# Attention of a four-stage transformer block: one written order of steps, or three

## The reference

```python
q, k, v = x @ wq, x @ wk, x @ wv             # 32 query heads, 8 key and value heads, 32 wide
q, k = rope(q), rope(k)                      # two layouts of the rotation, one per layer
scores = einsum('bqhd,bkhd->bhqk', q, k) / sqrt(32) + causal_mask
attn = softmax(scores, axis=-1)
out = einsum('bhqk,bkhd->bqhd', attn, v).reshape(b, s, 1024) @ wo
```

## Time and profile before

| | us |
|---|---|
| three runs | 3035.17, 3039.46, 3039.74 |
| median | 3039.46 |
| the profiled execution | 3036.84 |
| its span, first to last instruction | 3035.1 |
| TensorE busy | 2620.5 (86%) |
| VectorE busy | 1819.1 (60%) |
| ScalarE, GpSimd busy | 1081.8, 1123.2 |
| mean granted TensorE clock | 0.935 |

### The profile page before, as it was taken

The page is one execution under the profiler, slowest core; times in us unless marked ns, Lnnn a source line. Parts: engine busy times, 40 slices in busy tenths (PEclk is TensorE's granted clock), DMA queues, the critical chain, the costliest instruction groups (busy, mean ns, idle before and its releaser), DMA issues. The chain is left out here.

```text
span 3035.1 us, 50649 instructions
## 1 busy us (share of the span) xinstructions
PE 2620.5 (86%) x15056; PEld 1810.9 (60%) x15056; DVE 1819.1 (60%) x4485; ACT 1081.8 (36%) x2317; POOL 1123.2 (37%) x801
## 2 busy tenths in 40 slices
PE   7799997889998799653768999988799996996999
PEld 6556653655654588542645555545556553885887
DVE  5577775547776433688764666764577774225453
ACT  2155454135555211352511445552155454002000
POOL 7265653445664100000043555636265552001111
PEclk9999998999999899766979999989899998998999
DMA  4223221323231421000233323222323223433111
GB/s 149 87 81 104 64 75 63 117 71 104 77 86 42 161 69 55 0 0 7 83 132 95 106 61 93 73 83 74 90 81 103 64 75 112 146 131 146 63 69 42
DMA packets 121079, 252.95 MB, mean 83 GB/s; under 512 B 12720, under 2 KB 39728, under 8 KB 120880
## 3 DMA queue, kind: packets, MB, share of 16 engines
q1 hardware_dynamic: 120912, 251.03, 25.9%
HBM read 166.57 MB, written 84.41 MB: 83 GB/s over the span
## 5 line engine op out<-in xcount | busy, mean ns | idle before, releaser
L605 ACT ACTIVATE a_prob<-a_pst 128x512 f32<-128x512 f32 (+3 forms) x1536 | 660.7, 493 | 581.8 <-PE a_pst L886 576.2
L698 DVE CUSTOM_DVE_ANT_0 a_psh<-a_psh,a_edge 128x128 f32<-128x128 f32 (+3 forms) x1024 | 479.5, 518 | 247.7 <-PE a_psh L839 218.8
L839 PE MATMUL a_psh<-a_kst,a_qst 127*128 127x512 f32 (+3 forms) x1536 | 494.6, 371 | 79.4 <-DMA a_qst<-q 52.7
L886 PE MATMUL a_pst<-a_qst,a_kst 128*128 128x512 f32 (+2 forms) x1536 | 490.1, 374 | 22.7 <-DMA a_qst<-rowmax 17.8
L509 POOL TENSOR_TENSOR a_prob<-a_prob 128x2048 f32<-128x2048 f32 (+1 forms) x96 | 405.6, 4226 | 241.6 <-PE a_ppv L902 241.6
L839 PEld LDWEIGHTS a_psh<-a_kst,a_qst 127*128 127x128 f32 x1536 | 272.1, 191 | 321.9 <-DVE a_mx L701 104.7
L701 DVE TENSOR_REDUCE a_mx<-a_psh 128x1 f32<-128x512 f32 x512 | 328.2, 685 | 117.3 <-PE a_psh L839 116.4
L886 PEld LDWEIGHTS a_pst<-a_qst,a_kst 128*128 128x128 f32 x1536 | 289.4, 195 | 164.2 <-ACT a_prob L605 105.0
L902 PE MATMUL a_ppv<-a_prob,a_vg 128*32 128x512 f32 (+3 forms) x3072 | 319.8, 503 | 0.0
L915 PE MATMUL a_pden<-a_prob,a_ones 128*32 128x512 f32 (+3 forms) x2304 | 220.4, 475 | 13.8 <-POOL a_prob L509 13.8
L494 POOL TENSOR_SCALAR_AFFINE_SELECT a_prob<-a_prob 128x512 f32<-128x512 f32 x256 | 162.4, 640 | 184.7 <-ACT a_prob L605 184.3
(11 more groups left out here) (228 smaller groups left out, 4222.5 us busy)
## 6 DMA issues: line engine op xcount, KB each, us to landing
a_qst<-q SPq DMA_DIRECT2D x192, 256.0 KB, 4.4
a_wraw<-in_wqkv SPq DMA_DIRECT2D x52, 512.0 KB, 4.3
q<-a_stg_hi SPq DMA_DIRECT2D x64, 256.0 KB, 2.1
q<-a_stg_lo SPq DMA_DIRECT2D x64, 256.0 KB, 2.4
a_kst<-kT SPq DMA_DIRECT2D x96, 128.0 KB, 2.6
oT<-a_oT SPq DMA_DIRECT2D x32, 256.0 KB, 2.4
oT<-a_vT SPq DMA_DIRECT2D x32, 256.0 KB, 2.9
h_oraw<-oT SPq DMA_DIRECT2D x16, 512.0 KB, 4.0
```

The lines of the kernel that those rows point to most:

```text
L605: act.activation(prob[k % len(prob)][:, h, off:], pst[:, (k * GH + h) % 3, off:], ACT.Exp, scale=scale).then_inc(s["exp_done"], 1)
L698: part = dve.tensor_tensor_reduce(scores, scores, edge[:, BANK - n:], 1.0, 2 * MASKED, ALU.add, ALU.max, mx_hq[kc][:, h, qt:qt + 1])
L839: mm = pe.matmul(psh[:, at, i * n:(i + 1) * n], qst[par][0:P - 1, h, qt * P:(qt + 1) * P], kst[par][0:P - 1, kc * BANK:kc * BANK + n], sta ...
L886: pe.matmul(pst[:, (k * GH + h) % 3, off:], kst[par][:, ki * P:(ki + 1) * P], qst[par][:, h, qc * BANK + off:(qc + 1) * BANK], start=True, ...
```

## The change

Three orders are written out in place of one: `ORDER` for the looped groups, `ORDER_6` for group 6 and `ORDER_7` for group 7. `body7` is now `ORDER_7` without its `X` and `P` steps. Each list holds the same steps as before, in other places; no instruction, tile or semaphore is added or removed. `iteration` goes, `iterations` returns the lists, `parsed` reads `n` as the next batch and lets a list have no `S`.

In `ORDER`, `NORM:0` moves from behind `P:1.3` at the group's end to behind `ST:6.3`, the seventh key tile; the `S` start behind `P:0.0`; `ST:11.3` stands ahead of `P:1.1`; `VG` and `NORM:1` come a few steps earlier. In `ORDER_6` four `S` stand ahead of `ST:0.0`, and `NORM:0` at the end of unit 7. In `ORDER_7` `XL:0` to `XL:3` spread over the first units, each of the x steps has a written place, `NORM:0` stands in unit 10, and all eight `P:n` come at the end, behind `D:11`.

```diff
--- before.py
+++ after.py
@@ -75,39 +75,72 @@
 
 
 ORDER = """
-    P:0.0 P:0.1
-    ST:0.0 WL ST:0.1 ST:0.2 S P:0.2 ST:0.3 P:0.3
-    ST:1.0 ST:1.1 P:0.4 ST:1.2 S HI:1 ST:1.3 P:0.5
-    ST:2.0 ST:2.1 P:0.6 LO:1 S P:0.7 ST:2.2 S ST:2.3
-    ST:3.0 V:0 D:0 S S ST:3.1 ST:3.2 S ST:3.3 V:1
-    ST:4.0 ST:4.1 RS:1 ST:4.2 HI:0 S S D:1 ST:4.3 LO:0
-    ST:5.0 S ST:5.1 S V:2 V:3 D:2 D:3 S ST:5.2 S ST:5.3 S V:4 S
-    ST:6.0 S S ST:6.1 ST:6.2 S ST:6.3 V:5
-    ST:7.0 S ST:7.1 SUM:4+5 S ST:7.2 S ST:7.3 S V:6 SUM:6+7 D:4+5 S
-    ST:8.0 S ST:8.1 S RS:0 ST:8.2 S ST:8.3 S
-    ST:9.0 V:7 S S ST:9.1 ST:9.2 ST:9.3 S D:6+7 S
-    ST:10.0 ST:10.1 S V:8 S SUM:8+9 ST:10.2 S ST:10.3 V:9 S
-    ST:11.0 S ST:11.1 ST:11.2 P:1.0 P:1.1 ST:11.3 S P:1.2 S D:8+9 WS V:10 V:11 RK D:10 D:11 MT P:1.3
-      NORM:0 P:1.4 P:1.5 P:1.6 P:1.7 NORM:1 VG
+    P:0.0 S P:0.1
+    ST:0.0 WL ST:0.1 ST:0.2 S P:0.2 S ST:0.3
+    ST:1.0 P:0.3 S ST:1.1 P:0.4 HI:1 S P:0.5 ST:1.2 LO:1 ST:1.3
+    ST:2.0 S P:0.6 S ST:2.1 P:0.7 S ST:2.2 ST:2.3
+    ST:3.0 V:0 D:0 V:1 RS:1 ST:3.1 ST:3.2 S ST:3.3 S S
+    ST:4.0 HI:0 ST:4.1 ST:4.2 D:1 V:2 ST:4.3 S S
+    ST:5.0 S ST:5.1 D:2 V:3 S S ST:5.2 ST:5.3 LO:0 S
+    ST:6.0 D:3 V:4 S ST:6.1 S ST:6.2 ST:6.3 NORM:0 V:5 SUM:4+5
+    ST:7.0 S S ST:7.1 S ST:7.2 ST:7.3 V:6 D:4+5
+    ST:8.0 SUM:6+7 S RS:0 ST:8.1 ST:8.2 S S ST:8.3 S
+    ST:9.0 V:7 S ST:9.1 ST:9.2 S S ST:9.3 D:6+7
+    ST:10.0 S S V:8 SUM:8+9 ST:10.1 S S ST:10.2 V:9 S ST:10.3
+    ST:11.0 S ST:11.1 P:1.0 ST:11.2 S ST:11.3 P:1.1 RK S WS P:1.2 S D:8+9 V:10 V:11 D:10 D:11 MT P:1.3 VG
+      P:1.4 P:1.5 NORM:1 P:1.6 P:1.7
 """
 
+ORDER_6 = """
+    S S S S
+    ST:0.0 ST:0.1 ST:0.2 ST:0.3 HI:1
+    ST:1.0 S ST:1.1 ST:1.2 S S LO:1 S V:0 ST:1.3 S
+    ST:2.0 ST:2.1 D:0 ST:2.2 ST:2.3
+    ST:3.0 V:1 ST:3.1 S ST:3.2 ST:3.3 D:1
+    ST:4.0 V:2 RS:1 ST:4.1 S ST:4.2 ST:4.3 D:2 V:3 S
+    ST:5.0 ST:5.1 S S ST:5.2 D:3 S ST:5.3 S
+    ST:6.0 ST:6.1 S S V:4 S ST:6.2 S ST:6.3 S
+    ST:7.0 S S ST:7.1 ST:7.2 SUM:4+5 ST:7.3 V:5 V:6 SUM:6+7 D:4+5 NORM:0
+    ST:8.0 S ST:8.1 S ST:8.2 S ST:8.3 S
+    ST:9.0 V:7 ST:9.1 S ST:9.2 S ST:9.3 S D:6+7 V:8 S S
+    ST:10.0 S ST:10.1 ST:10.2 SUM:8+9 V:9 S ST:10.3 S S S
+    ST:11.0 ST:11.1 ST:11.2 S ST:11.3 V:10 D:8+9 D:10 V:11 D:11 MT NORM:1
+"""
+
+ORDER_7 = """
+    ST:0.0 ST:0.1 ST:0.2 XL:0 ST:0.3 XL:1
+    ST:1.0 ST:1.1 ST:1.2 ST:1.3 V:0 XL:2
+    ST:2.0 ST:2.1 ST:2.2 XS:0 XS:1 XN:0 V:1 ST:2.3
+    ST:3.0 XS:2 ST:3.1 ST:3.2 ST:3.3 XT:0 XL:3 D:0 XN:1 XC:0 XN:2 V:2
+    ST:4.0 D:1 ST:4.1 ST:4.2 XS:3 XT:1 XC:1 D:2 XL:4 V:3 ST:4.3
+    ST:5.0 ST:5.1 XS:4 XL:5 D:3 XT:2 XN:3 XC:2 ST:5.2 V:4 XN:4 ST:5.3 SUM:4+5
+    ST:6.0 ST:6.1 ST:6.2 XS:5 XT:3 XL:6 XC:3 ST:6.3
+    ST:7.0 V:5 ST:7.1 XS:6 XL:7 XN:5 XT:4 XC:4 ST:7.2 ST:7.3 D:4+5 V:6 XN:6
+    ST:8.0 SUM:6+7 ST:8.1 XT:5 XS:7 XC:5 ST:8.2 V:7 XN:7 ST:8.3
+    ST:9.0 ST:9.1 ST:9.2 XT:6 XC:6 ST:9.3 D:6+7 V:8
+    ST:10.0 ST:10.1 NORM:0 ST:10.2 SUM:8+9 ST:10.3
+    ST:11.0 ST:11.1 XT:7 XC:7 ST:11.2 ST:11.3 V:9 D:8+9 V:10 D:10 V:11 D:11 P:n.0 NORM:1 P:n.1 P:n.2
+      P:n.3 P:n.4 P:n.5 P:n.6 P:n.7
+"""
+
 
 def parsed(text):
 
 
     steps, k = [], 0
+    number = lambda x: "next" if x == "n" else int(x)
     for word in text.split():
         what, _, rest = word.partition(":")
         if what == "S":
             steps.append(("S", k))
             k += 1
         elif what in ("ST", "P"):
-            steps.append((what, *(int(x) for x in rest.split("."))))
+            steps.append((what, *(number(x) for x in rest.split("."))))
         elif what in ("D", "SUM"):
             steps.append((what, tuple(int(x) for x in rest.split("+"))))
         else:
             steps.append((what, int(rest or 0)))
-    assert k == len(USES)
+    assert k in (0, len(USES))
     return steps
 
 
@@ -118,42 +151,17 @@
 SUMS = [step[1] for step in STEPS if step[0] == "SUM"]
 
 
-def iteration(full_s=True, proj=True, ahead=False):
-
-
-
-
-    left_out = set() if proj else {"P", "WL", "WS", "RK", "VG"}
-    if not full_s:
-        left_out |= {"S", "MT"}
-    order = []
-    for step in STEPS:
-        what, k = step[:2]
-        if what in ("HI", "LO", "RS") and not (proj if k == 0 else full_s):
-            continue
-        if what not in left_out:
-            order.append(step)
-    if ahead:
-
-
-        def put(step, *others):
-            order[order.index(step) + 1:order.index(step) + 1] = others
-
-        for i in range(PIECES):
-            put(("ST", 11, 1) if i < 3 else ("ST", 11, 3) if i < 6 else ("V", 10), ("P", "next", i))
-        for i in range(ST_):
-            put(max([("ST", i + 1, 0)] + [("XN", i - 2)] * (i > 1) + [("XC", i - 4)] * (i > 3), key=order.index), ("XS", i))
-            put(max(("V", i), ("XS", i), key=order.index), ("XN", i))
-            put(max([("ST", i + 3, 1), ("XN", i)] + [("XC", i - 1)] * (i > 0), key=order.index), ("XT", i))
-            late = max(("V", i + 2), ("XT", i), key=order.index)
-            put(late, ("XC", i), *[("XL", i + NX_AHEAD)] * (i + NX_AHEAD < ST_))
-        pieces = iter(range(PIECES))
-        order = [("P", "next", next(pieces)) if step[0] == "P" else step for step in order]
-        order = [("XL", i) for i in range(NX_AHEAD)] + order
-        for i in range(ST_):
-            assert sorted(("XS", "XN", "XT", "XC"), key=lambda w: order.index((w, i))) == ["XS", "XN", "XT", "XC"]
-            assert i == 0 or order.index(("XC", i - 1)) < order.index(("XC", i))
-    return order
+def iterations():
+
+
+
+
+    body, body6, ahead7 = parsed(ORDER), parsed(ORDER_6), parsed(ORDER_7)
+    body7 = [step for step in ahead7 if step[0][0] not in "XP"]
+    for order in (body6, ahead7):
+        assert [step[1] for step in order if step[0] == "D"] == DENS
+        assert [step[1] for step in order if step[0] == "SUM"] == SUMS
+    return (body, parsed(ORDER)), body6, body7, ahead7
 
 
 def prologue():
@@ -235,8 +243,7 @@
 
     ZT0, W0, SH0, R0, E0, V0, D0, AC0, N0, ST0, DMA0 = 4, 2, 1, 4, 3, 2, ND, 1, 1, 2, 16
 
-    pro, bodies, body6, body7 = prologue(), (iteration(), iteration()), iteration(proj=False), iteration(False, False)
-    ahead7 = iteration(False, False, True)
+    pro, (bodies, body6, body7, ahead7) = prologue(), iterations()
     plan_pro, U_PRO, _ = bank_plan(pro, (0, 1), spare=(2, 3, 4, 5))
     plan, kept, settled = {}, None, False
     while not settled:
```

## The result

The changed kernel takes 3051.44 us (median; 3049.2 to 3053.68), the one before 3039.6 beside it: ratio 1.0037, 95% interval 1.0024 to 1.0051. It is slower by 11.8 us, where 3050 was forecast. The profiled execution's span is 3050.9 us against 3035.1: 15.8 more.

The account below looks back on a forecast made before the run. TensorE was taken to bound the looped groups, busy 46.1 of 47.4 us. Looped groups +8, heads +11, group 0 +6, group 6 +22 and group 7 -36 sum to +11 us: 3050 median, range 3005 to 3072.

Parts of the forecast that it names:

- looped groups: Groups 0 to 5: MT's wait -0.56, NORM:0 beside a sum +0.6, S:11 +0.3; +0.35 each, +8 us over 24.
- group 6: Four groups: +0.7 at head and S:11, S:26 waiting 3.0 behind NORM:0, lower clock; +22 us in all.
- group 7: With x tiles: earlier x loads, fewer waits for x tiles, 58.2 us against 76.3; -18 each, -36 for two.
- the last group 7: Group 7 of the last batch, with nothing behind it on VectorE: 0, 1 us either way.
- group 0: S:0 now stands before P:0.1 and three ST, which follow the queries' transfer: +1.4, four times, +6 us (4 to 11).
- the heads: Loop's head, groups 2 and 4: S:2 wanted earlier, its wait 0.97 to 2.3 us; +1.4 at eight heads, +11.
- In two heads VectorE's gap is longer; the shift is the same: Two loop heads whose groups took 54.3 us: the early scores add the same +1.4 us as at the others.
- The 1.7 for the clock: Group 6: TensorE's clock drops for 3.5 us after the wait of S:26, costing 1.7 us.
- The +0.7 for the head and `S:11`: Group 6: four scores ahead of ST:0.0, partly given back, and a longer second wait of S:11; together +0.7 us.
- B: Rival: neither NORM:0 in group 6 nor XN:6 in group 7 meets a pair sum; -16, 3023 us; chance 0.28.
- C: Rival: maxima have more slack, no steady group waits for NORM:0 or queries; -37, 3002 us; chance 0.12.
- D: Rival: lower clock follows every head's 2.3 us wait, 1.7 more in eight; group 7 gives only 12; 3076 us; chance 0.11.

Follow-up runs that it names:

- mt_back: The kernel of s_back with P:1.1 ahead of ST:11.3 again in the looped groups; 3033.83 us, 0.9986 of the kernel before.
- s_back: The changed kernel with the scores of the looped groups' first key tiles back in their old places, NORM:0 still in the seventh; 3016.8 us.
- seven_new: The kernel before with only the new order of group 7 with x tiles; 3009.86 us, ratio 0.9907.
- norm_early: The kernel of seven_new with NORM:0 moved from the tail to behind ST:6.0, the seventh key tile of the old order; 3132.43 us, 1.0297.
- best2: s_back with old-order group 6 but NORM:0 behind ST:9.0, old-order last group 7, SUM:6+7 behind XS:7 in the other group 7; 2994.54 us, 0.9867.
- six_norm: The changed kernel with NORM:0 of group 6 behind ST:9.0 instead of beside SUM:6+7; 3035.47 us, 0.9987 of the kernel before.
- best3: The kernel of best2 with S:30 and S:31 of group 6 moved behind V:8; 2994.75 us, 0.9855 of the kernel before.

## Why the prediction was right, and where it was not

**The sum.** Forecast +11, measured +11.8 in the medians and +15.6 in the traces. Its parts, forecast against the table: looped groups with their heads and groups 0 +25 against +23.9; group 6 +22 against +22.5; group 7 -36 against -34.8; the last group 7 "0, 1 either way" against +4.0. The last term was mis-sized. In each of its two stretches TensorE waits 2.5 us for GpSimd's pair sums (1.37 and 1.09 in group 15), which the new list makes closer to their use; before it waited 0.2 and not at all. The two stretches together took 60.7 to 64.0 us in the six traces with the old list there and 64.3 to 67.7 in the eight with the new one.

The agreement of the first part is luck. Up to the first group 1 of each batch the time grew by 11.6 us (the third batch with the other stages in it), where the forecast's terms for group 0 make 7; behind it by 12.3, where the others make 18. Group 0 was too small and the heads were too large, and the two cancelled.

**Looped groups.** `MT`'s wait went in all groups, as mt_back shows the other way round. In the changed kernel L714 took 0.82 us and not 1.60, and `MT` follows without a wait (VectorE and TensorE, end of group 3, against the earlier trace rows):

```profile
325.52 0.82 DVE L714 TENSOR_TENSOR a_mx<-a_mx 128x16 f32<-128x16 f32 x1 [0.17 <-issue]
...
326.56 0.28 PE L855 MATMUL a_psh<-a_ident,a_mx 128*32 128x128 f32 x1
```

L759 took 1.2 to 1.5 us and ended 0.55 behind the sum, as said, but of the scores behind it only `S:24` waited, 0.27 and not 0.6 in all. `S:11` went the other way: its waits in the 24 groups grew from 4.3 to 19.3 us together, 0.6 a group, and 0.5 in groups 1 to 5, where 0.3 was forecast. Groups 1 and 3 of the batches came to +0.46 each (379.3 against 375.6 for eight), forecast +0.35. The mechanisms held and, group 0 apart, their sizes were within 0.4 us a group.

**The heads.** Forecast `S:2` waiting 2.3 in place of 0.97; it waited 1.67 to 2.06 in the six heads with the short gap, because it was wanted at 3.5 to 3.6 us of the group and got its bank at 5.3 to 5.7 (3.3 and 5.5 in the forecast). The eight groups grew by 8.4 us, forecast 11 and the share of the other terms (2.8). "In two heads VectorE's gap is longer; the shift is the same" was wrong: TensorE waited 4.71 and 4.89 there before, 4.41 and 4.78 after. VectorE came to the branch 3.0 us earlier and the score was wanted 3.9 earlier, as at the other heads, but the gap itself was 1.2 and 1.0 shorter, measured from the start of the operation ahead of it; why, stays open. (Of these two groups one took 54.3 us before and the other 53.3, where the forecast has 54.3 for both.) The forecast also said that an order which comes to the branch earlier hides none of the gap. s_back comes to it 3 us earlier on VectorE, leaves the score where it was, and hides the gap from TensorE in six heads of eight. It is the early score that exposes it. The sentence of the page "Runtime: NRT & Kernel Launch" of the Trainium skill (Instruction fetch mechanics) on branches out of the fetched window is compatible with the gap of 2.6 and 5.2 us; no run separates a fetch from another cost of the branch.

**Group 0.** Forecast +6. This term was the furthest off. In the first batch `MT` came at 61.2 us of the group and not at 58.2: 3.0, twice the forecast's 1.4. In the other three it came 2.2, 1.5 and 7.6 later, 14.3 in all, beyond the forecast's own bound of 11. The part of 1.4 is there (`P:0.1` and three `ST` behind a wait that ends at the same 135.2, and the earlier trace rows has 135.27). What was left out is the second half of the queries: `LO:1` hangs on the pieces behind that wait, so `S:11` waits 2.57 (0.70 before) where s_back, with the scores late, has 0.09. In the last batch it waits 2.43, and there the clock falls too: 0.77 granted from 2200 to 2215, where the kernel before has 1.00 from 2200 to 2233.

**Group 6.** Forecast `S:26` waiting 3.0 behind a multiplication of over 3.5; it waited 3.05 behind 4.21. The 1.7 for the clock did not come in the first batch: from 460.30 on the granted clock was 1.00. Behind the same wait (3.04 to 3.07) of the other three groups it was 0.50 to 0.60 for 3.5 us, and in two of them it had been 0.66 in the first 5 us as well, which the forecast did not have. The +0.7 for the head and `S:11` does not follow from the terms that stand beside it; the waits ahead of `S:26` came to 0.9 more than before (0.83, 0.49, 0.28 and 1.33 against 0.56, 0.47 and 1.03). So the size of the whole was right, and the clock's share of it came in three groups of four.

**Group 7.** `XT:0` found its tile (seven_new shows what it costs when it doesn't), `XN:6` met the sum and took 4.92 us, `XT:6` waited 3.55 (forecast 4.5) with the lower clock behind it (0.50 for 3.5 us), the last piece began at 51.5 and ended at 52.4 (51).

**The rivals.** B and C needed the two collisions to fail. Both happened in every batch that has them (4.19 to 4.22 us in the four groups 6, 4.92 and 4.94 in the two groups 7). D needed the lower clock behind every head, and it came behind four of eight: in group 4 the granted clock was 0.55 for 3.5 us behind the wait and in group 2 it was 1.00 throughout, with the same wait, so it does not follow from the wait's length alone. Windows of the changed kernel: group 4, and 3.5 us behind the waits of `S:2` in group 4 and of `S:26` in group 6.

```profile
331.95:382.38 50.43, 48.11 (x315) 29.30 (x313) 35.16 (x99) 25.21 (x55) 27.92 (x20) 0.97 0.29 82
335.50:339.00 3.50, 3.50 (x11) 3.02 (x12) 2.03 (x9) 1.26 (x3) 0.64 (x1) 0.55 0.00 0
460.30:463.80 3.50, 3.50 (x24) 1.71 (x28) 2.81 (x9) 1.75 (x4) 0.09 (x1) 1.00 0.21 80
```

**What the forecast did not see.** It weighed each edit against the kernel before and not against the others. `NORM:0` out of the tail was worth having; the early scores spent that gain at the heads and 17 us in the groups 0 (s_back against the change, up to group 1: 2.6, 4.5, 1.5 and 7.9; the third with the other stages in it). The net was right and the two large terms of opposite sign in it were not named.

## What to carry to other kernels

When a long step is moved on an engine that empties a few banks, count how long the producer can go on behind its new place. Here three banks hold scores. The shorter the time from the place of `NORM:0` to the moment at which the fourth score behind it is wanted, the longer TensorE waited there. Read from the timelines (us of the group; in group 6 counted from its first score or `ST`, whichever is first):

```
run, group             place of NORM:0         fourth score wanted     slack    its wait
the change, group 6    27.6 (beside a sum)     S:26 at 29.5            1.9      3.05
norm_early, group 2    21.5 (beside a sum)     S:18 at 24.9            3.4      2.86
best2, group 6         27.3                    S:30 at 30.9            3.6      1.70
six_norm, group 6      29.3                    S:30 at 33.7            4.4      0.49
best3, group 6         27.4                    S:30 at 32.4            5.0      0.27
s_back, group 2        22.8 (beside a sum)     S:22 at 28.2            5.4      none
```

Slack and wait add up to 4.9 to 6.3 us in the five rows with a wait, since what VectorE has to do behind `NORM:0` is not the same in all of them. So the table orders these lists; it does not give a threshold for another one.

And undo the edits of a change one at a time before it is judged: of three new lists here one was worth 28 us, and of the two main edits in the looped list one had to be kept and one taken out. The one to keep is not good by itself: in the old list the same move cost 123 us.
